# Routed tiles cut by 32 rows: 18 tiles with an upper half of two quarters, in place of 21 tiles of two halves

## The reference, cut to what matters

```python
logits = xt @ gate_w.T                       # xt is [592, 256], 15 logits for each token
scores = softmax(logits)
topk_w, topk_idx = top_k(scores, 3)          # every token goes to 3 of 15 experts
topk_w = topk_w / (sum(topk_w) + 1e-20)
comb = zeros(T, E).at[arange(T)[:, None], topk_idx].add(topk_w)
h = einsum('td,efd->etf', xt, fc1_w) + fc1_b # 256 -> 512 for each expert
xh, g = h[..., :256], h[..., 256:]
a = gelu(g) * xh * geglu_mult
yexp = einsum('etf,edf->etd', a, fc2_w) + fc2_b   # 256 -> 256
y = einsum('etd,te->td', yexp, comb)
return y + shared_expert(xt)
```

## Time and profile before

| what | us |
|---|---|
| median of 3 runs | 211.79 |
| lowest, highest | 211.71, 212.29 |
| the profiled execution's own time | 211.57 |
| its span, first to last instruction | 209.8 |
| outside the span | 1.8 |
| TensorE busy in the span | 199.2 |
| mean granted TensorE clock | 0.992 |

### The profile page before, as it was taken

The page is one execution under the profiler, slowest core; times in us unless marked ns, Lnnn a source line. Parts: engine busy times, 40 slices in busy tenths (PEclk is TensorE's granted clock), DMA queues, the critical chain, the costliest instruction groups (busy, mean ns, idle before and its releaser), DMA issues.

```text
span 209.8 us, 4431 instructions
## 1 busy us (share of the span) xinstructions
PE 199.2 (95%) x1559; PEld 124.7 (59%) x1559; DVE 113.2 (54%) x313; ACT 94.4 (45%) x219; POOL 121.5 (58%) x148
## 2 busy tenths in 40 slices
PE   7999998999998899999998999999999999999981
PEld 4776676678786675776775753355444555445630
DVE  6685697868863444264799953642344332231034
ACT  2004565477868373564557762333332433235024
POOL 0040079869989857929999877216665552347100
PEclk9999999999999999999999999999999999999996
DMA  6999999960000399922220034228985321112483
GB/s 199 391 416 314 402 415 417 425 270 0 6 3 3 97 379 376 417 83 64 78 71 22 0 100 108 78 92 304 366 326 164 92 75 53 50 50 91 145 248 116
DMA packets 13822, 38.32 MB, mean 183 GB/s; under 512 B 2697, under 2 KB 4618, under 8 KB 13802
## 3 DMA queue, kind: packets, MB, share of 16 engines
q1 hardware_dynamic: 11786, 32.54, 42.4%
q0 software_dynamic: 2016, 5.51, 8.4%
HBM read 29.27 MB, written 4.06 MB: 159 GB/s over the span
## 4 chain that ended last, share of the span: by engine, by line
PE 77%; DVE 8%; DMA 6%; issue 2%; ACT 2%; POOL 2%; SPq 1%; POOLq 0%; DVEq 0%; ACTq 0%
PE ps L383 66%; PE ps L1874 3%; PE ps L1672 2%; DMA wres<-y_dram 2%; PE ps L1914 2%; PE ps L1687 2%; DMA embed_sb<-embed 1%; POOL y_dram L668 1%; DMA embed_sb<-x_dram,gather_i 1%; DMA y_dram<-ln_mem,dest_i 1%; PE ps L1603 1%; PE ps L1530 1%; DVE over L1270 1%; POOL embed_sb L659 1%; ACT ln_mem L905 1%
## 5 line engine op out<-in xcount | busy, mean ns | idle before, releaser
L383 PE MATMUL ps<-wres,cT 128*64 (+1 forms) x360 | 63.1, 469 | 0.0
L383 PEld LDWEIGHTS ps<-wres,cT 128*64 128x64 f32 (+1 forms) x360 | 25.4, 131 | 27.7 <-issue 20.5
L668 POOL DMA_INDIRECT y_dram<-ln_mem,dest_i x21 | 20.6, 982 | 26.8 <-ACT ln_mem L875 23.4
L426 POOL TENSOR_TENSOR wres<-wres,fac_mem 128x512 f32<-128x512 f32 x22 | 27.2, 1271 | 4.3 <-DVE ln_rs L1033 4.3
L659 POOL DMA_INDIRECT embed_sb<-x_dram,gather_i x21 | 20.3, 968 | 8.2 <-issue 5.2
L1406 DVE TENSOR_TENSOR fac_mem<-ps,h 128x256 f32<-128x256 f32 x21 | 8.9, 423 | 24.0 <-ACT h L869 24.0
L869 ACT ACTIVATE h<-ps 128x256 f32<-128x256 f32 x21 | 8.0, 383 | 28.5 <-PE ps L383 28.5
L383 PE MATMUL ps<-h,stage 128*128 128x296 f32 x64 | 18.2, 422 | 0.7 <-DVE xn L1384 0.6
L1413 DVE COPY cT<-ps 128x256 f32<-128x256 f32 x21 | 8.8, 424 | 15.6 <-PE ps L383 15.6
L875 ACT ACTIVATE ln_mem<-ps 128x256 f32<-128x256 f32 x21 | 8.0, 383 | 15.8 <-PE ps L383 15.8
L383 PEld LDWEIGHTS ps<-h,stage 128*128 128x128 f32 x64 | 11.6, 190 | 5.4 <-DVE xn L1384 1.0
(11 more groups left out here) (215 smaller groups left out, 379.9 us busy)
## 6 DMA issues: line engine op xcount, KB each, us to landing
wres<-experts SPq DMA_DIRECT2D x15, 768.0 KB, 13.5
fac_mem<-experts SPq DMA_DIRECT2D x11, 256.0 KB, 8.1
wres<-ut SPq DMA_DIRECT2D x3, 768.0 KB, 8.8
embed_sb<-embed SPq DMA_DIRECT2D x5, 416.0 KB, 5.6
stage<-shared SPq DMA_DIRECT2D x2, 771.0 KB, 16.4
stage<-wres SPq DMA_DIRECT2D x2, 512.0 KB
wres<-y_dram SPq DMA_DIRECT2D x2, 512.0 KB, 4.2
wres<-y_dram SPq DMA_DIRECT2D x2, 384.0 KB, 6.3
```

Of the source, the lines that this page charges most:

```text
L383: return nc.tensor.matmul(o, w, x, start=start, stop=stop)
L426: nc.gpsimd.tensor_tensor(w1(e, c), w1(e, c), row, ALU.subtract).then_inc(less_done, 1)
L668: pool.indirect_dma_start(out=y_dram[:, :], out_offset=bass.IndirectOffsetOnAxis(ap=dest_i[:, column(i):column(i) + 1], axis=0), in_=ys[:, ...
```

## The change

A group is still 64 rows in the lower half, but the upper half of a tile is now two quarters of `TQ = 32` rows, each of its own expert. The worst case is 55 + 15 = 70 quarters, so `NT = 18` tiles. An expert's first quarter and an odd quarter lie in upper halves, pairs of quarters in lower ones. `NB = 19` of the 36 upper quarters have an expert known only on the chip; their weights are copied, two quarters (a pair) at a time, `NPAIR = 10` pairs, through rings of three (first product) and four (second product) pairs of buffers. The order of the tiles (`COLUMNS`) puts the pairs at tiles 4, 6, 8, 10, 12, 13, 14, 15, 16 and 17 (`AT`). `first` and `second` issue three products for each chunk in place of two: one with 64 stationary columns and two with 32. The slot arithmetic on VectorE and a second table of owners grow with it.

```diff
-TM = 64
-PT = P // TM
-NT = ((T * TOPK - E) // TM + E + PT - 1) // PT
+TM, TQ = 64, 32
+PT, PQ = P // TM, P // TQ
+
+QUARTERS = (T * TOPK - E) // TQ + E
+NT = (QUARTERS + PQ - 1) // PQ
 NTT = NT * PT
+
+NB = max(QUARTERS - E - PT * NT, E)
+NPAIR = (NB + 1) // 2
+assert NB + E <= PT * NT
 SUMS = 32
...
-NCOPY = NT - E
-NOVER = NTT - E
-RT_END = 28
+COLUMNS = (10, 11, 12, 13, 0, 14, 1, 15, 2, 16, 3, 17, 4, 5, 6, 7, 8, 9)
+assert sorted(COLUMNS) == list(range(NT))
+AT = [COLUMNS.index(n) for n in range(NPAIR)]
+W1_PAIRS, W2_PAIRS = 3, 4
+RT_END = 42
 NXG = 6
...
-            sp.wait_ge(own_done, 1)
+            sp.wait_ge(own_done, 2)
             all_scaled(sp)
-            for k in range(NCOPY):
-                e = sp.value_load(owner_i[0:1, NT + k:NT + k + 1], min_val=0, max_val=E - 1)
-                sp.wait_ge(f1_mm, 2 * k + 1)
-                sp.dma_start(copy_w1[k], wres[:, bass.ds(e * WC, W1C)]).then_inc(ld_copy, 16)
-                sp.dma_start(copy_w2[k], wres[:, bass.ds(e * WC + W1C, W2C)]).then_inc(ld_copy, 16)
+            sp.wait_ge(f1_mm, 1)
+            copied = {}
+
+            def copy_first(n):
+                copied[n] = [sp.value_load(owner_i[0:1, NT + v:NT + v + 1], min_val=0, max_val=E - 1)
+                             for v in range(PT * n, min(PT * n + PT, NB))]
+                if n >= W1_PAIRS:
+                    sp.wait_ge(f1_mm, AT[n - W1_PAIRS] + 1)
+                for h, e in enumerate(copied[n]):
+                    sp.dma_start(copy_w1[PT * (n % W1_PAIRS) + h], wres[:, bass.ds(e * WC, W1C)]) \
+                        .then_inc(ld_cw1[n % W1_PAIRS], 16)
+
+            def copy_second(n):
+                if n >= W2_PAIRS:
+                    sp.wait_ge(y2_mm, AT[n - W2_PAIRS] + 1)
+                for h, e in enumerate(copied[n]):
+                    sp.dma_start(copy_w2[PT * (n % W2_PAIRS) + h], wres[:, bass.ds(e * WC + W1C, W2C)]) \
+                        .then_inc(ld_cw2[n % W2_PAIRS], 16)
+                del copied[n]
+
+            sp.wait_ge(y_done, NH * DC)
+            for n in range(NPAIR):
+                copy_first(n)
+                if 0 < n < NPAIR - 2:
+                    copy_second(n - 1)
+            copy_second(NPAIR - 3)
+            copy_second(NPAIR - 2)
+            copy_second(NPAIR - 1)
             sp.wait_ge(st_zero, 16)
             rows_written(sp)
@@ -887,7 +923,7 @@
...
+                nc.vector.tensor_tensor(rank[:, :], rank[:, :], flat, ALU.mult).then_inc(rt, 1)
...
             def slots():
-                held, extra, upto, before, far = (over[:, i] for i in range(5))
                 posn = ps[:, 3, 0:(TT + 1) * E]
+                places = posn[:, 0:TT * E].rearrange("p (t e) -> p t e", t=TT)
                 dve.wait_ge(pos_mm, 1)
-                nc.vector.tensor_scalar(over_i[:, :], posn[:, TT * E:], float(TM - 1), None, ALU.add).then_inc(rt, 1)
-                nc.vector.tensor_tensor(slot[:, :].rearrange("p (t e) -> p t e", t=TT),
-                                        posn[:, 0:TT * E].rearrange("p (t e) -> p t e", t=TT),
+                nc.vector.tensor_scalar(over_i[:, 0], posn[:, TT * E:], 1.0, -1.0, ALU.max, ALU.add).then_inc(rt, 1)
+                nc.vector.tensor_tensor(slot[:, :].rearrange("p (t e) -> p t e", t=TT), places,
                                         rte[:, C_128E:C_128E + E].unsqueeze(1).to_broadcast([P, TT, E]),
                                         ALU.add).then_inc(rt, 1)
                 dve.wait_ge(rt, 3)
-                nc.vector.tensor_scalar(over_i[:, :], over_i[:, :], TM.bit_length() - 1, None,
+                nc.vector.tensor_scalar(over_i[:, 1], over_i[:, 0], TM.bit_length() - 1, None,
                                         ALU.arith_shift_right).then_inc(rt, 1)
-                dve.wait_ge(rt, 4)
-                nc.vector.scalar_tensor_tensor(extra, over_i[:, :], 1.0, rte[:, C_VALID:C_VALID + E],
-                                               ALU.max, ALU.subtract).then_inc(rt, 1)
-                dve.wait_ge(rt, 5)
-                nc.vector.tensor_tensor_scan(upto, extra, zrow[:, 0:E], 0.0, ALU.add, ALU.add).then_inc(rt, 1)
+                nc.vector.tensor_scalar(over_i[:, 2], over_i[:, 0], TQ.bit_length() - 1, 1,
+                                        ALU.arith_shift_right, ALU.bitwise_and).then_inc(rt, 1)
                 dve.wait_ge(rt, 6)
-                nc.vector.tensor_tensor(before, upto, extra, ALU.subtract).then_inc(rt, 1)
+                nc.vector.tensor_copy(counts, over_i[:, 1:3]).then_inc(rt, 1)
                 dve.wait_ge(rt, 7)
-                nc.vector.scalar_tensor_tensor(far, before, float(TM), rte[:, C_CA:C_CA + E],
+                nc.vector.tensor_tensor_scan(upto.rearrange("p v e -> p (v e)"), rte[:, C_RESET:C_RESET + 2 * E],
+                                             counts.rearrange("p v e -> p (v e)"), 0.0, ALU.mult, ALU.add).then_inc(rt, 1)
+                nc.vector.tensor_scalar(least, counts[:, 0], float(TM), TQ - 0.5, ALU.mult, ALU.add).then_inc(rt, 1)
+                dve.wait_ge(rt, 8)
+                nc.vector.tensor_tensor(before, upto, counts, ALU.subtract).then_inc(rt, 1)
+                nc.vector.tensor_scalar(pairs2[:, :], upto[:, 0, E - 1:E], float(NT), 2.0, ALU.max, ALU.mult).then_inc(rt, 1)
+                dve.wait_ge(rt, 9)
+                nc.vector.tensor_tensor(odd_t[:, :].rearrange("p (t e) -> p t e", t=TT), places,
+                                        least.unsqueeze(1).to_broadcast([P, TT, E]), ALU.is_gt).then_inc(rt, 1)
+                dve.wait_ge(rt, 10)
+                nc.vector.scalar_tensor_tensor(far, before[:, 0], float(TM), rte[:, C_CA:C_CA + E],
                                                ALU.mult, ALU.add).then_inc(rt, 1)
-                dve.wait_ge(rt, 8)
+                nc.vector.scalar_tensor_tensor(odd_far, upto[:, 0], -2.0, before[:, 1], ALU.mult, ALU.add).then_inc(rt, 1)
+                dve.wait_ge(rt, 13)
                 nc.vector.scalar_tensor_tensor(
-                    jump[:, :].rearrange("p (t e) -> p t e", t=TT),
-                    posn[:, 0:TT * E].rearrange("p (t e) -> p t e", t=TT), TM - 0.5,
+                    jump[:, :].rearrange("p (t e) -> p t e", t=TT), places, TQ - 0.5,
                     far.unsqueeze(1).to_broadcast([P, TT, E]), ALU.is_gt, ALU.mult).then_inc(rt, 1)
-                dve.wait_ge(rt, 9)
+                dve.wait_ge(rt, 14)
+                nc.vector.tensor_scalar(odd_far, odd_far, pairs2[:, 0:1], float(TQ), ALU.add, ALU.mult).then_inc(rt, 1)
+                dve.wait_ge(rt, 15)
                 nc.vector.tensor_tensor(slot[:, :], slot[:, :], jump[:, :], ALU.add).then_inc(rt, 1)
-                dve.wait_ge(rt, 10)
-                nc.vector.tensor_tensor(jump[:, :], slot[:, :], flat, ALU.mult).then_inc(rt, 1)
+                dve.wait_ge(rt, 16)
+                nc.vector.tensor_tensor(odd_t[:, :].rearrange("p (t e) -> p t e", t=TT),
+                                        odd_t[:, :].rearrange("p (t e) -> p t e", t=TT),
+                                        odd_far.unsqueeze(1).to_broadcast([P, TT, E]), ALU.mult).then_inc(rt, 1)
+                dve.wait_ge(rt, 18)
+                nc.vector.tensor_tensor(slot[:, :], slot[:, :], odd_t[:, :], ALU.add).then_inc(rt, 1)
             def choose():
-                dve.wait_ge(rt, 11)
-                pick_of(0, jump[:, :].rearrange("p (t e) -> p t e", t=TT))
-                dve.wait_ge(rt, 14)
+                dve.wait_ge(rt, 19)
+                pick_of(0, slot[:, :].rearrange("p (t e) -> p t e", t=TT))
...
+            def owners_copied():
+
+                nc.vector.tensor_scalar(ends[:, 0], upto[:, 0], 2.0, None, ALU.mult).then_inc(rt, 1)
+                nc.vector.tensor_scalar(ends[:, 1], upto[:, 1], pairs2[:, 0:1], None, ALU.add).then_inc(rt, 1)
+                dve.wait_ge(rt, 38)
+                nc.vector.tensor_tensor(owner_b[:, :, :],
+                                        ends.rearrange("p v e -> p (v e)").unsqueeze(1).to_broadcast([P, NB, 2 * E]),
+                                        rte[:, C_TILE + NT:C_TILE + NT + NB].unsqueeze(2).to_broadcast([P, NB, 2 * E]),
+                                        ALU.is_le).then_inc(rt, 1)
+                dve.wait_ge(rt, 39)
+                nc.vector.tensor_reduce(owner_f[:, NT:], owner_b[:, :, :], AX.X, ALU.add).then_inc(rt, 1)
+                dve.wait_ge(rt, 40)
+                nc.vector.tensor_scalar(wrap[:, :], owner_f[:, NT:], E - 0.5, -float(E), ALU.is_ge, ALU.mult).then_inc(rt, 1)
+                dve.wait_ge(rt, 41)
+                nc.vector.tensor_tensor(wrap[:, :], wrap[:, :], owner_f[:, NT:], ALU.add).then_inc(rt, 1)
                 dve.wait_ge(rt, RT_END)
-                nc.vector.tensor_scalar(owner_i[:, :], owner_f[:, :], E - 1.0, None,
-                                        ALU.min).then_inc(own_done, 1)
+                nc.vector.tensor_scalar(owner_i[:, NT:], wrap[:, :], E - 1.0, None, ALU.min).then_inc(own_done, 1)
...
```

(65 more changed lines are left out.)

49 lines of the change are left out of this document (29 added, 20 removed).

## The result

The changed kernel takes 274.74 us in the median of 4 runs (274.38 to 275.04), against 212.04 (211.71 to 213.0) for the kernel before on the same chip: 1.295 times as long, 95% interval 1.290 to 1.300. The profiled execution took 275.04, with a span of 273.2 against 209.8. One run of a later experiment (e4, 229.88 us, at a granted clock of 0.937) was in a slower state of the chip and is left out of its median. In the new file the products (line 383 before) are recorded with line 396, `tile_transposed` with 1947 and `gated_transposed` with 2000 (2002 where an edit adds two lines).

The account below looks back on a forecast made before the run. PE was taken to bound the kernel, at 3.17 us a tile. Tiles +55, stall +5.4, clock +2, chain +1.1 and end -1 gave +62.5 and so 274 us; range 255 to 292, likeliest case 262 to 283.

Parts of the forecast that it names:

- Shapes take turns by blocks: PE's tile products: 64- and 32-column blocks never overlap, 6.75 us a tile instead of 3.17, +55 us; likeliest case, chance 0.72.
- Passes alternate singly: Rival on PE's tile products: single passes of the shapes alternate, doubling the switches, +9 us on tiles, 283 us; chance 0.12.
- The stall: PE at `first(4)` waits for the first pair of copied weights, issued behind `comb17`: 5.4 us, bounds 3 to 7.
- The clock: PE's work after the stall runs partly at 1.2 instead of 2.4 GHz: +2 us, range 0 to 4.
- The chain on DVE: DVE's slot arithmetic ahead of the tiles grows, delaying the first gather and tile 0: +1.1 us, range 0 to 1.8.
- the +1.5 for `slots`: Within DVE's chain: added slot steps and masking of `rank`, less a removed line, together +0.4 to +2.1, taken as 1.5.
- The end: Behind the tiles: GpSimd's scatters keep up, -1.3, but PE's own work limits the gain; counted as -1 us.
- Later copies hidden: Copies after the first pair: 4 us a pair against 13.5 for two tiles, so no further wait.
- a tile without the 0.03 of each first pass: Low bound for the tiles: switches cost nothing extra behind the first pass, 6.3 us a tile, 113 us, 8 less.
- the low ends of the terms: Likeliest case's lowest values: tiles 113, stall 3, clock 0, chain 0; said to give 262 us together.
- The overlap rival: Three products share PE's array despite shapes: tiles 57.4 us, stall 9.4 at `first(4)`, +3.3, 215 us; chance 0.12.
- Its faster sister: Rival: products overlap and copies land 3 us earlier, stall 6 and clock 1 at `first(4)`, 210.7 us; chance 0.04.

Follow-up runs that it names:

- e4: Changed kernel with all products 32 columns wide (constant expert for a quarter of rows) and the first six copies ahead of the routing-weight stores: 224.05 us, ratio 1.036.
- e2: Changed kernel with the 64-column products of both chunks first in each tile, then the 32-column ones: 266.63 us, ratio 1.242.
- e5: Kernel before, 21 tiles, with each tile's upper group computed as two 32-column products with the same weights, output unchanged: 285.77 us, ratio 1.336.
- e6: Kernel before with four 32-column products per chunk, rows 32 to 63 using a constant expert's weights: 218.93 us, ratio 1.024.
- e1: Changed kernel with the lower group also as two 32-column products, rows 32 to 63 using a constant expert's weights: 228.48 us, ratio 1.062.
- e3: Changed kernel with SyncE's comb17 stores, wait and read back moved behind the copies of the first three pairs: 268.46 us, ratio 1.249.
- e7: As e6, but rows 32 to 63 take weights of expert (i + 7) modulo 15, differing from the upper group's: 219.09 us, ratio 1.024.

## Why the prediction was right

Forecast 274.0, measured 274.74. By its own steps:

- **Shapes take turns by blocks.** Right, and this is 54.5 of the 63.4 us. Forecast for a tile 6.75, measured 6.75; +55 forecast, +54.5 measured. The choice rested on three rows where a shape changed at a cost of 0.1. e2 shows the price of a change of shape, e5 that mixing alone gives the whole, e6 that it is gone when all products have one shape. The Trainium skill, TensorEngine Tiling (Array Packing), section Tiling Modes, says that a change of the tiling mode drains TensorE, and all of these agree with it; what the traces show directly is only that nothing starts for 0.10 and that the shapes never overlap. The Trainium skill, TensorE: Matmul & The Clock Gate, section Part 3, has further tiles of the array start some 4 ns apart and run at the same time; here that is so within a shape, where the 32-column pair starts 0.01 us apart, and not between the two shapes.
- **But the changes of shape are the smaller part.** Eight changes of shape at 0.13 are 1.04 us of a tile. The other 2.54 of the 6.75 - 3.17 is that half an array idles: the 64-column product streams alone for as long as two used to together, and then the 32-column pair for as long again. Even e2, with half of the changes, keeps that. The forecast's sum has it in its first term, 4 blocks of two passes in place of 2.
- **Passes alternate singly** (283): no. Both passes of a product follow each other in the timeline above.
- **The stall.** Place and releaser right, 5.4 forecast, 6.9 measured. PE reached `first(4)` at 142.7 and not 143.4, since it began earlier; the copy landed at 149.4 and not 148.8. It was issued at 144.3, 0.5 earlier than reckoned, and its data had passed soon after 148, as the sum would then have it (144.3 + 1.2 + 2.7 = 148.2). What the sum did not have is the 1.2 from there to the recorded landing, and the 0.24 from the landing to PE's first product.
- **The clock.** +2 forecast, +2.5 measured; the level is 0.50, as in the earlier trace rows, and it held for some 5 us of products after the wait of 6.9.
- **The chain on DVE.** +1.1 forecast, +0.3 measured at the first product, and even that is not clear of noise. In the six traces with the new chain tile 0 starts between 124.48 and 125.51, in the four with the old one between 124.73 and 125.31, with means of 124.97 and 125.09. In the two traces compared here the chain already began 0.5 later (105.60 instead of 105.11); from its start to the first hot table it grew by 0.27, and the smaller hot tables gave 0.35 back. The mis-sized term is the +1.5 for `slots`, in both directions: the masking of `rank` is recorded at 1.12 where 0.27 was counted, and `slots` itself, from 107.26 to 110.97, takes 3.71 where it took 4.12 (105.60 to 109.73), though it has more steps.
- **The end.** -1 forecast, -0.7 measured.
- **Later copies hidden.** Right: no further wait for one. e4 shows how near the limit is when a tile takes 4.1 (73.8 / 18) in place of 6.75.

The small errors of stall (+1.5), clock (+0.5), tiles (-0.5), chain (-0.8) and end (+0.3) nearly cancel, so 0.7 us off is in part luck, and better than the terms deserve. Two bounds in the prediction don't follow from its own terms either: a tile without the 0.03 of each first pass is 6.5 and not 6.3 (117 us for the tiles, not 113), and the low ends of the terms add up to 260, not 262. Neither touches the forecast.

The overlap rival gave 215 with a stall of 9.4. The nearest thing to it that could be run is e1, where all products overlap: 225 on 212, with a stall of 12.6. Its faster sister at 210.7 needed a stall of 6.

## What to carry to other kernels

Before you count on products filling the array side by side, look at whether they have one shape. Products of 64 columns ran beside each other here, and so did those of 32, but one of 64 next to two of 32 made them take turns, which doubled the tile (3.17 to 6.75 us) while the count of tiles fell by a seventh. Look in the trace at the starts of neighbouring passes, and at any place where the shape changes, before you trade uniform tiles for fewer ones. And when a transfer stands behind a serial errand of its queue, put the transfer first if its consumer waits: e3 got 9.7 us back by order alone.

## What the runs showed of the hardware that I had not expected

**Four products of 32 columns side by side complete late.** In e6, and in e1 and e4, the recorded products run ahead of what waits for them. PE records all 16 products of `first(0)` from 125.04 on (e6's timeline; PE, then ScalarE's gate, which needs only that tile):

```profile
125.04 1.92 PE L383 MATMUL ps<-wres,cT 128*32 x16
131.25 3.64 PE L383 MATMUL ps<-wres,cT 128*32 x32 [1.70 <-issue]
```

```profile
129.31 0.38 ACT L869 ACTIVATE h<-ps 128x256 f32<-128x256 f32 x1 [3.27 <-PE ps L383]
148.73 0.38 ACT L869 ACTIVATE h<-ps 128x256 f32<-128x256 f32 x1 [4.18 <-remote]
```

The gate of tile 0 starts 2.35 us behind the end of the recorded products, that of tile 7 (148.73) 2.9 behind; the profile names "remote" there, which means that it found nobody on this core who ended the wait. Of the 21 gates, 8 are late by 0.7 to 3.1, 10 by no more than 0.1. In the kernel before, in the changed kernel and in e5, where at most two products run at once, it is 0.05 for every tile. Then PE shows idle time that nothing ends:

```profile
PE ps L383 <- issue: 4.4, 7, 1.7
```

These 4.4 us are close to e6's 5 us over the kernel before on the same chip (between the two traces, the stretch of the tiles is 6.3 longer: 73.2 against 66.9). The likeliest reading is that the array really takes longer than the modelled ends say for four at once, 0.25 to 0.3 us a tile on the mean (5 or 6.3 over 21), and that the idle time is it catching up. That is argued, not shown: the granted clock is 1.00 throughout the tiles, e7 rules out the choice of weights, and why some tiles are 3 us late and others not at all stays open. For readers of traces: where ends are modelled, check them against the start of the engine that waits.

**Not every difference of size makes products take turns.** In the kernel before, the sums behind the tiles (`last_sums`) have in each step two products of 32 columns over 32 rows and one of 16 over 16. Groups of instructions from 202.2 to 203.6 (count, busy us, mean ns):

```profile
L383 PE MATMUL ps<-wres,embed_sb 32*32 32x256 f32 x12 | 1.5, 378 | 0.0
L383 PE MATMUL ps<-wres,embed_sb 16*16 16x256 f32 x6 | 1.5, 376 | 0.0
```

Both sizes are spread over the same 1.5 us, and the three passes of a step start within 0.02. These 18 passes one behind another, at 0.21, would be 3.8. So the 16-column products ran beside those with 32, and it is the pair of 64 and 32 columns, not any unequal pair, that these runs show taking turns. Other pairs were not tried.
